# The tail of a two-layer graph network: unrolled in a new order, neighbour sums transposed, edge tiles loaded in contiguous halves

## The reference, cut to what matters

```python
# layer 1 (the code's L0)
qkv = layer_norm(x, g1, be1) @ w_qkv
scores = jnp.where(adj != 0, einsum('nhd,mhd->hnm', q, k) * SCALE, -inf)
x = x + softmax(scores) @ v @ w_proj + b_proj
x = x + gelu(layer_norm(x, g2, be2) @ w1 + b1) @ w2 + b2
# layer 2 (the code's L1): s has one value per row, H = 64
h = x @ Wt.T + bt
s = leaky_relu(h @ Wa.T + ba, 0.2)
w = softmax(where(adj > 0, s, NEG), axis=1)
y = x + (w @ h) @ Wp.T + bp
out = gamma * normalise(y) + beta
```

## Time and profile before

| | |
|---|---|
| median of 3 runs | 1380.0 us |
| the profiled execution | 1379.69 us, its span 1377.9 us |
| before the tail (phases 1 and 2) | 1076.1 us |
| head of the tail, edge loads being issued | 21.2 us |
| layer 1, eight chunks | 150.6 us |
| layer 2, eight chunks | 109.4 us |
| after the last neighbour sum | 20.6 us |

### The profile page before, as it was taken

One profiled execution on the slowest core, in us unless ns is written; L12 is line 12 of the kernel. 1 busy time (PEld: TensorE's weight loads), 2 busy tenths in 40 slices (PEclk: granted clock), 3 DMA queues, 4 the chain that ended last, 5 costly groups with the idle time before them and its releaser, 6 DMA issues.

```text
span 1377.9 us, 32788 instructions
## 1 busy us (share of the span) xinstructions
PE 1203.9 (87%) x12296; PEld 401.1 (29%) x12296; DVE 1138.8 (83%) x1599; ACT 1050.0 (76%) x1183; POOL 876.6 (64%) x913
## 2 busy tenths in 40 slices
PE   5547999999999999999999999999999277788994
PEld 3321111111111111111111111111111055567984
DVE  6656999999999999999999999999999145553544
ACT  4546999999999999999999999999999122220000
POOL 5675777777777777777777777777777022220323
PEclk9777999999999999999999999999999678899997
DMA  5002232332333233233224224323321831104992
GB/s 162 1 18 77 100 132 93 108 135 97 108 121 112 93 125 122 93 113 134 93 93 149 98 93 134 113 93 112 135 93 55 221 107 46 46 0 119 300 303 72
DMA packets 104276, 152.30 MB, mean 111 GB/s; under 512 B 4992, under 2 KB 84544, under 8 KB 95936
## 3 DMA queue, kind: packets, MB, share of 16 engines
q1 hardware_dynamic: 83456, 139.81, 31.1%
q10 hardware_dynamic: 20672, 10.49, 3.0%
HBM read 110.43 MB, written 39.85 MB: 109 GB/s over the span
## 4 chain that ended last, share of the span: by engine, by line
ACT 61%; issue 14%; DVE 9%; PE 7%; POOL 5%; ACTq 2%; POOLq 1%; DMA 0%; DVEq 0%; SPq 0%
ACT probs L1048 35%; ACT probs L1042 26%; POOL probs L948 2%; PE ps L469 2%; ACTq L277 1%; DVE probs L1151 1%; PE ps L1251 1%; POOL adj_in L580 1%; PE ps L1191 1%; DVE probs L1077 1%; DVE acc_sb L1159 1%; DVE v_sb L384 1%; PE ps L455 1%; DVE probs L1089 1%; POOL v_sb L250 1%
## 5 line engine op out<-in xcount | busy, mean ns | idle before, releaser
L1151 DVE SCALAR_TENSOR_TENSOR probs<-m,ps 128x512 f32<-128x512 bf16 (+1 forms) x1024 | 928.9, 951 | 33.2 <-PE ps L1251 15.0
L1048 ACT ACTIVATE probs<-probs 128x1536 f32<-128x1536 f32 x512 | 867.3, 1695 | 0.9
L984 POOL TENSOR_TENSOR probs<-probs,m 128x512 f32<-128x512 f32 x512 | 596.0, 1164 | 226.4 <-ACT probs L1042 197.2
L1264 PE MATMUL ps<-probs,v_sb 128*17 128x512 f32 x4096 | 539.2, 599 | 0.2 <-ACT probs L1048 0.2
L1251 PE MATMUL ps<-kq 32*128 32x512 bf16 x6144 | 426.3, 380 | 38.2 <-DVE probs L1151 9.7
L1042 ACT ACTIVATE probs<-ps 128x512 f32<-128x512 f32 x512 | 411.0, 803 | 23.4 <-PE ps L1251 22.7
L1251 PEld LDWEIGHTS ps<-kq 32*128 32x128 bf16 x6144 | 114.7, 93 | 565.3 <-ACT probs L1042 499.0
L963 POOL TENSOR_SCALAR m<-adj_in 128x512 bf16<-128x512 int32 x256 | 157.3, 615 | 4.0 <-issue 3.9
L1264 PEld LDWEIGHTS ps<-probs,v_sb 128*17 128x17 f32 x4096 | 68.2, 95 | 218.7 <-issue 210.2
L710 PE MATMUL ps<-probs,kq 128*128 128x193 bf16 x1024 | 88.8, 246 | 0.0
L710 PEld LDWEIGHTS ps<-probs,kq 128*128 128x128 bf16 x1024 | 86.0, 97 | 1.1 <-DMA kq<-mask_t 0.2
(11 more groups left out here) (126 smaller groups left out, 641.1 us busy)
## 6 DMA issues: line engine op xcount, KB each, us to landing
adj_in<-in_adj_t SPq DMA_DIRECT2D x64, 1024.0 KB, 5.6
mask_t<-m SPq DMA_DIRECT2D x64, 512.0 KB, 2.9
kq<-mask_t SPq DMA_DIRECT2D x12, 2048.0 KB, 17.3
kq<-mask_t ACTq DMA_DIRECT2D x4, 2048.0 KB, 17.3
attn_t<-acc_sb SPq DMA_DIRECT2D x16, 256.0 KB, 6.4
tail_words<-attn_t SPq DMA_DIRECT2D x8, 512.0 KB, 3.4
probs<-in_x SPq DMA_DIRECT2D x8, 256.0 KB, 4.2
tail_words<-in_x SPq DMA_DIRECT2D x8, 256.0 KB, 3.6
```

What stands on the lines that cost most here:

```text
L984: nc.gpsimd.tensor_tensor(pr, pr, m01[:, (k // 2) % MRING, :], ALU.mult).then_inc(postmasked, 1)
L1048: nc.scalar.activation(pr, pr, ACT.Exp, scale=UNIT).then_inc(exped, 1)
L1151: nc.vector.scalar_tensor_tensor(out=pr, in0=m.to_broadcast([P, n, CH]), scalar=1.0, in1=ps[:, b:b + n, :], op0=ALU.subtract, op1=ALU.add)\
L1264: last = nc.tensor.matmul(ps[RT * hh:RT * hh + VW, 6 + g, :], v_sb[:, t, h * VW:(h + 1) * VW], probs[:, k % SLOTS, hh // 2, (hh % 2) * CH: ...
```

## The change

The tail is written anew.

1. **Edge tiles.** All sixteen loads are issued by SyncE. A load takes 16 of the 32 tiles of a chunk with all 512 columns: 128 pieces of 16 KB. Five of them fit (`ERING`), where four did before, and the attention sums of a chunk (`acc`, `xr`, `xb`) have two buffers.
2. **Order of layer 1.** No hardware loops. `normalise_att` stands a step earlier, `turn_acc` stands ahead of `turn_h2`, and the two copies of `hidden_parts` are ScalarE's (`hidden_high`, `hidden_middle`). `s_row` comes from a 65th column of the weight (`wt_aug`), so a multiply, a reduction and an addition on VectorE go. `ff1` uses two banks in turn. GpSimd adds up `h` (`hidden_sum`).
3. **Layer 2.** The features are stationary and the edge tile moves, 512 columns at a time: `sums_high` (128 columns of `h3`, one matmul per tile), `sums_low` (64 columns, even and odd tiles into the lower and the upper half of the output partitions) and the degree (`one_col`, 32 columns, four tiles into four groups of 32 output partitions). The sums come out transposed, so the transpose and the per-row weighting ahead of the projection go; the weights are applied to the projection's result.
4. The barrier between layer 1 and layer 2 goes: the first half of chunk 0 is summed ahead of the last chunk's `hidden`.
5. Transposed weights come ready from the host (`wt_t`, `wp2`); `Wa` is brought through `Wt` on TensorE once.

```diff
-        edges = kq[:, 0:2 * NT * CH].rearrange("p (s t q) -> p s t q", s=2, t=NT)
+        edges = kq[:, :].rearrange("p (s t q) -> p s t q", s=5, t=NT // 2)
...
+        def load_edges(sp, n):
+            if n >= ERING:
+                sp.wait_ge(edges_used, n - ERING + 1)
+            j, half = n // 2, n % 2
+            sp.dma_start(edges[:, n % ERING, :, :], m_dram[j, :, half * HALF:(half + 1) * HALF, :])\
+                .then_inc(edges_in[n % ERING], 16)
...
-            for u in range(2):
-                for half in range(2):
-                    q = slice(half * CH // 2, (half + 1) * CH // 2)
-                    act.dma_start(edges[:, u, :, q], m_dram[u, :, :, q]).then_inc(edges_in[u][half], 16)
...
+            for i in range(NC):
+                if i >= 2:
+                    hidden_low(i - 2)
+                if i + 1 < NC:
+                    first_sum(i + 1)
+                    normalise_x1(i + 1)
+                second_sum(i)
+                if i + 2 < NC:
+                    normalise_att(i + 2)
+                if i >= 1:
+                    hidden(i - 1)
+                    hidden_parts(i - 1)
...
+            def sums_high(n):
+                j, half = n // 2, n % 2
+                pe.wait_ge(edges_in[n % ERING], 16 * (n // ERING + 1))
+                if half == 0 and j >= 2:
+                    pe.wait_ge(s_made, j - 1)
+                    pe.wait_ge(deg_copied, j - 1)
+                for t in range(half * HALF, (half + 1) * HALF):
+                    nc.tensor.matmul(ps[:, BANK_A[j % 2], :], h3[:, t, 0:2 * HID], edges[:, n % ERING, t % HALF, :],
+                                     start=t == 0, stop=t == NT - 1)
+
+            def sums_low(n):
+                j, half = n // 2, n % 2
+                for t in range(half * HALF, (half + 1) * HALF):
+                    r = (t % 2) * HID
+                    nc.tensor.matmul(ps[r:r + HID, BANK_B[j % 2], :], h3[:, t, 2 * HID:3 * HID],
+                                     edges[:, n % ERING, t % HALF, :], start=t < 2, stop=t >= NT - 2)
+                for t in range(half * HALF, (half + 1) * HALF):
+                    r = (t % 4) * RT
+                    last = nc.tensor.matmul(ps[r:r + RT, BANK_D[j % 2], :], one_col[:, :],
+                                            edges[:, n % ERING, t % HALF, :], start=t < 4, stop=t >= NT - 4)
+                last.then_inc(edges_used, 1)
...
-                    for t in range(NT):
-                        last = nc.tensor.matmul(sums(u)[:, s, 0:AGG],
-                                                edges[:, u, t, s * P:(s + 1) * P], h3[:, t, 0:AGG],
-                                                start=t == 0, stop=t == NT - 1)
```

More of the change, by code:

```diff
@@ L398, in hidden_parts @@
-                nc.vector.scalar_tensor_tensor(out=s_row[:, at], in0=s_row[:, at], scalar=0.2,
-                                               in1=s_row[:, at], op0=ALU.mult, op1=ALU.max)\
-                    .then_inc(hid_step, 1)
-            def step(c, first, last):
-                if not last:
-                    normalise_att(c + 1)
-                    first_sum(c + 1)
-                if not first:
-                    hidden(c - 1)
-                if not last:
-                    normalise_x1(c + 1)
-                second_sum(c)
-                if not first:
-                    hidden_parts(c - 1)
+                nc.vector.scalar_tensor_tensor(out=s_row[:, at], in0=hid[:, :, HID], scalar=0.2,
+                                               in1=hid[:, :, HID], op0=ALU.mult, op1=ALU.max)
@@ L427, in tail_tensor, with finish @@
+            def finish(j):
+                dve.wait_ge(yr_step, 2 * j + 2)
+                for s in range(SUB):
+                    last = nc.vector.tensor_scalar(y[:, s, :], y[:, s, :], ymv[:, s, 0:1], yrs[:, s:s + 1],
+                                                   ALU.subtract, ALU.mult)
+                last.then_inc(y_normed, 1)
+            for j in range(NC):
+                add_parts(j)
+                weights(j)
+                residual(j)
+                finish(j)
         def tail_tensor(pe):
@@ L483, in hidden @@
                 for s in range(SUB):
-                    last = nc.tensor.matmul(ps[:, B_HID, s * HID:(s + 1) * HID],
-                                            x2T[:, s * P:(s + 1) * P], wtT, start=True, stop=True)
+                    last = nc.tensor.matmul(ps[:, B_HID, s * (HID + 1):(s + 1) * (HID + 1)],
+                                            x2T[:, s * P:(s + 1) * P], wt_aug[:, 0:HID + 1], start=True, stop=True)
                 last.then_inc(hid_done, 1)
-            def step(c, first, last, ahead):
-                ff1(c, (0, 1))
-                if not last:
-                    turn_att(c + 1)
-                if not first:
-                    turn_rows(x2, B_X2, x2_made, x2_turned, c - 1)
-                ff1(c, (2, 3))
-                if not last:
-                    project(c + 1)
-                if not first:
-                    hidden(c - 1)
-                ff2(c)
-                if not last:
-                    turn_rows(h2, B_TURN, h2_made, h2_turned, c + 1)
-                if ahead:
-                    turn_acc(c + 2, not first)
             turn_acc(0)
@@ new lines, in tail_tensor @@
+            turn_h2(0)
+            for i in range(NC):
+                ff1(i, (0, 1))
+                if i + 1 < NC:
+                    turn_att(i + 1)
+                ff1(i, (2, 3))
+                if i + 1 < NC:
+                    project(i + 1)
+                if i >= 1:
+                    turn_x2(i - 1)
+                ff2(i)
+                if i + 2 < NC:
+                    turn_acc(i + 2)
+                if i + 1 < NC:
+                    turn_h2(i + 1)
+                if i >= 1:
+                    hidden(i - 1)
@@ new lines, in column_sums @@
+            def column_sums():
+                pe.wait_ge(hsum_made, NC)
+                pe.wait_ge(x2_made, NC)
+                for s in range(SUB):
+                    last = nc.tensor.matmul(ps[0:HID, B_OUT, 0:P], hsum[:, s, :], onesf,
+                                            start=s == 0, stop=s == SUB - 1)
+                last.then_inc(cs_done, 1)
+                pe.wait_ge(cs_copied, 1)
+                nc.tensor.matmul(ps[:, B_OUT, P:2 * P], csT[0:HID, :], wp2_sb[0:HID, :], start=True, stop=True)\
+                    .then_inc(csw_done, 1)
@@ new lines, in tail_tensor @@
+            pe.wait_ge(h_lo_made, NC // 2)
+            pe.wait_ge(gelu_made, NM * NC)
+            sums_high(0)
+            turn_x2(NC - 1)
+            sums_low(0)
+            hidden(NC - 1)
+            pe.wait_ge(h_lo_made, NC)
+            sums_high(1)
+            sums_low(1)
+            column_sums()
+            for j in range(1, NC):
+                sums_high(2 * j)
+                sums_low(2 * j)
+                project_sums(j - 1)
+                sums_high(2 * j + 1)
+                sums_low(2 * j + 1)
@@ L748, in gnn_kernel @@
+            project_sums(NC - 1)
         block = ctx.enter_context(nc.Block())
```

637 lines of the change are left out of this document (318 added, 319 removed).

## The result

The changed kernel takes **1321.95 us** (median of 4 runs, 1321.62 to 1323.13); the kernel before, on the same chip, 1379.57 (4 runs, 1378.61 to 1380.53). The ratio is 0.9584, 95% interval 0.9567 to 0.9600: 57.6 us less. 1321 was predicted.

What follows compares the result with a forecast made beforehand. Bound: loads holding ScalarE's queue in the head, a cross-engine chain in layer 1, TensorE in layer 2. Head -20.7, layer 1 -45, layer 2 +11, end -4: span 1319.1, time 1321 us; own range 1309 to 1331, overall 1305 to 1346.

Steps and rivals of the forecast that it cites:

- The head: Start of the tail: ScalarE no longer issues loads, so turn_acc starts at 1076.6, not 1097.32: 20.7 us less.
- A step: Layer 1: first step 13.0 us from half clock, others 11.35 instead of 19.32, chain and TensorE level, clock 1.00.
- First sum: Start of layer 2: step 7 starts at 1173.3, plus 9.3 of TensorE work, so first neighbour sum at 1182.6.
- The handover: Layer 1 to layer 2: first half to 1190.3, 3.3 us wait for last h, second half 6.3, column sums 1.7: 1201.6.
- A chunk: Layer 2: 12.04 us of matmuls, 0.6 for changes of group shape, 1.8 projection: 14.4; seven of 14.44 end at 1302.7.
- the 0.2 a change: Layer 2: alternative price for a change of group shape instead of 0.10; the sum would be some 5 us higher.
- Layer 2 gets slower: Layer 2: a chunk takes 14.4 us against 13.5 before, losing 0.9; first sum to last +11 us.
- The end: After the last sum: copy, addition, projections, weights, products, scaling and store take 16.4 us instead of 20.56: -4.
- The sum: Whole kernel: 1302.7 plus 16.4 gives a span of 1319.1, time 1320.9, so 1321 us.
- column groups do not overlap: Rival, layer 2: a chunk's TensorE work is 20.6 us instead of 12.04, 69 us more, 1390; chance 0.03.
- VectorE and GpSimd do stand in each other's way: Rival, layer 1: VectorE's split waits for GpSimd; missing by 2 us, seven steps lose 15: 1336; chance 0.15.
- only the head is won: Rival: layer 1 finds another chain of 18 us because VectorE's work is only moved: 1359; chance 0.06.

Runs made afterwards that it cites:

- Experiment 1: Kernel before, with only its first four edge loads moved from ScalarE's queue to SyncE, behind the last chunk's sums: 1360.38 us, ratio 0.9857.
- Experiments 3 and 9: Changed kernel with normalise_att back behind the splitting on VectorE: 1329.07 us; the same with the splitting's bf16 copies also back on VectorE: 1346.93 us.
- Experiment 8: Changed kernel with tiles 16 to 27 of the first chunk's second-half high sums run ahead of the wait for the last h: 1317.63 us.
- experiment 7: Changed kernel with each half's layer 2 work in two pieces of 8 tiles, so matmul shape changes six times a half instead of three: 1328.4 us.
- experiment 4: Changed kernel's head, layer 1 and loads, but neighbour sums as before: edge tiles stationary, 193 columns of h moving, sums transposed and projected: 1309.4 us, ratio 0.9488.
- experiment 5: Changed kernel with all 16 low matmuls of a half in one column group, so no two can run side by side: 1350.29 us, ratio 0.9787.
- experiment 12: experiment 4's kernel with the first chunk's sums as early as their tiles allow and GpSimd's first bias add behind VectorE's first h2: 1303.39 us, ratio 0.9441.
- experiment 2: Changed kernel with the low and degree matmuls of a half issued column group by column group instead of by turns: 1336.24 us.
- experiments 2, 5 and 6: The third of these: changed kernel with a half's 16 low matmuls in runs of four to one column group instead of by turns: 1322.9 us.

## Why the prediction was right, step by step

- **The head, -20.7.** Right, and shown by itself: the first transposes of sums start at 1077.08 (forecast 1076.6, with the attention 0.45 later), ff1(0) at 1092.62 (1092.2). Experiment 1 has it alone at 19.3.
- **A step, forecast as 13.0 for the first and 11.35 for the others.** Measured: 13.43 and 11.22. The forecast had chain and engine nearly level; the trace shows TensorE alone, at 11.19 busy. ff1's first pair took 1.99 and its second 1.72; the kernel before has the same pair of figures (1.98 at 1126.14, granted clock 1.00), and the prediction took the cheaper for both. Why the first is dearer no run shows. The others came in under the prices from the earlier trace rows, ff2 at 3.57 instead of 3.64, hidden at 0.84 instead of 0.91. Experiments 3 and 9 show what carried it: VectorE's order (7.1) and its share (with the order 25.0). First sum forecast for 1182.6, found at 1182.8: ff1(0) and the first step came 0.8 late together and the six steps 0.8 early, which is luck. That every other engine is busy for about half of the old layer 1 was misread: by the earlier trace rows it holds for VectorE (79 of 151 us), while ScalarE and GpSimd are at a quarter; the sum does not use it.
- **The handover.** hidden ended at 1190.51 (1190.3), the wait for h was 2.87 (3.3). Not in the sum: the clock. The second half's 15 high sums took 4.80 instead of 3.40. Experiment 8 got wait and clock back together, 4.3 us against 2.87 + 1.40. Column sums took 2.0 instead of 1.7, with a wait of 0.36 for ScalarE's copy between their two products.
- **A chunk, forecast as 14.44.** Measured: 14.65. The matmuls were priced right; the six changes of shape were priced at 0.10 and cost 0.113 (experiment 7), and the projection took 2.0 instead of 1.8: the one-column matmuls cost as much as those of 128 (0.98 against 1.00), so the price taken, at the dear end, was even short. Over seven chunks 1.5 us. At the 0.2 a change that the prediction weighed the sum would have been 5 us higher than it was, and too high. The Trainium skill, TensorEngine Tiling (Array Packing), Key Properties, says that changing the tiling mode drains TensorE; the trace agrees that a change costs something, at 0.113 us.
- **Layer 2 gets slower.** Right in sign, +13.5 against +11; the 2.5 us are the clock (1.4) and the chunks (1.5), less a shorter wait. Against the sums of before in a better order it is not 0.9 a chunk that is lost but 2.2 (experiment 4), because the 13.5 of before contained a wait.
- **The end, forecast as 16.4.** Measured: 15.8 from the last sum. The terms as written add up to 16.3, so 0.1 of the forecast is a slip.
- **The sum.** The last sum ended at 1305.5 (1302.7), 2.8 late, the end took 0.6 less, and the span came out 2.2 above the 1319.1 forecast. The median lies nearer, 0.95 above 1321, since the profiled execution was the slowest of the four. The mechanism held, stage by stage; that the hit is within 1 us is luck, and 2 to 3 us is what the forecast was good for.

The rivals: that column groups do not overlap fell with 1.85 and 0.98 in the first trace, and experiment 5 shows what would have been lost. VectorE and GpSimd do stand in each other's way: L505, ahead of the splitting, takes 1.12 us in the changed kernel with GpSimd beside it (from 1140.18 to 1141.30, GpSimd's L297 from 1140.00 to 1141.27), and 0.165 in its last step, and experiment 12 takes a delay of the same kind away at the head by moving GpSimd's work; hidden_low nevertheless ended 1.1 us ahead of the first sum, inside the cover. That only the head is won fell with the 11.22. What failed outright is an expectation behind the prediction: in experiment 2 all overlap was to go once the groups went apart (+65), and 14.3 did. That matmuls of one group can wait while another group's go ahead was missing from the theory; it stands on four run lengths and the degree's order now (experiments 2, 5 and 6), though what sets it at about four a group, no run shows.

## What to carry to other kernels

Price a transposed layout by the columns that TensorE streams plus about 0.11 us for each change of group shape, and set that against the old layout without its avoidable waits, not against its measured pace: here the old sums, better placed, win by 12.5 us, although their end is 4.7 longer. In a chain that crosses engines, put on the engine that everybody waits for first what the next engine needs, and its own housekeeping after it. And keep large loads off the queue of an engine that computes: who issues them was worth 19.3 us. Once SyncE issues them, the shape of their pieces was worth nothing.

## What the runs showed of the hardware

- Matmuls of 64-column groups need not alternate to run side by side: runs of four still pair up (1.87 us for 16), runs of eight in part (2.74), a single run of sixteen not at all (3.57). With 32-column groups, runs of four over four groups still lie four abreast (1.01 us for 16), so the limit of about four goes by the group.
- A wait of 2.87 us in dense work was followed by 1.4 us more in the next sums (granted clock 0.50 at first), half the wait again.
- Loads of a 2 MB half reached 382 GB/s over 10 us as contiguous halves and 310 as 512-byte pieces, the DMA engines busy for 1.00 and 1.17 by the profile's count. By itself such a contiguous load held the issuing queue for 0.50 us; a pair of 512-byte halves held it for 3.3 to 5.5.
- A matmul with 128 stationary columns and one moving column in fp32 cost as much as one with 128 moving columns: eight records in 0.98 and in 1.00 us.
- Four multiplications of 128 columns on VectorE took 3.02 us with GpSimd's additions of 512 columns beside them, and 1.11 without.
